# Ranks of edges from keys along the free dimension in place of transposed one-hots

## The chip, the cores and the metric

One core of a Trainium2 chip runs the whole program. The metric is the device time of one execution in microseconds. TensorE (PE), VectorE (DVE), ScalarE (ACT), GpSimd (POOL) and SyncE (SP) run their own instruction streams and meet at semaphores; data moves between DRAM and SBUF by DMA.

## The reference, cut to what matters

Four graph layers follow each other on 12,500 nodes of 32 features and 200,000 edges (padded to 128 x 1568). Edges come sorted by destination, not by source. The last layer needs sums over the edges of each source, so the kernel sorts the edges by source itself. Nothing in the reference is called a rank; what matters of it is

```python
edge_index = jnp.stack([src, dst])
...
x = x + _L1_gnn_ref(h, edge_index, 12500)      # msgs = x[src]; out = segment_sum(msgs, dst)
...
x = x + _L3_gnn_ref(h, edge_index, L3_gnn_w, L3_gnn_fc_w, L3_gnn_fc_b, L3_gnn_bias)
# in it: seg_max, seg_sum and segment_sum over src
```

The rank of an edge is its place in the order by source: the number of edges with a smaller source, plus the number of earlier edges with the same source.

## The kernel before

The 1568 columns of edges are handled in chunks of 16 (`CH`), a chunk holds 128 x 16 edges, and a chunk is ranked in four groups of four columns (`GR`, `GROUPS`). The edges are in two lists by the parity of their chunk, `ROWS` and `PTRS`, with 49 chunks (`PAIRS`) each. A key is split into `lo` (key mod 128) and `hi` (key div 128, 98 values). VectorE makes two one-hots of a chunk, `hot_lo` 128 x 16 x 128 (L1095) and `hot_hi` 128 x 16 x 98 (L1097), by comparing with `iota_ps`, a row of numbers in PSUM. A table `place_ps`, 128 x 98, holds for each key where its next edge goes; it starts from the prefix sums of the counts, and each group adds its own edges (`hot_lo` transposed times `hot_hi`).

For a group the kernel before does this (class `Ranks`). TensorE transposes the four `hot_lo` (L1002); ScalarE copies the result twice, to bf16 and to f32 (L1067, L1068). TensorE multiplies the transposed one-hots with each other, which tells which edges share `lo`: four blocks within a column, with a triangle added so that only earlier rows count (L1035, L1038), and three calls between columns (L1042). ScalarE copies these (L1081, L1082). TensorE counts the group on into `place_ps` (L1049, L1051), ScalarE copies that (L1085), and TensorE then makes for each of the four columns a 128 x 98 product of table and equal keys (L1011, L1014, L1015) in which VectorE picks each edge's `hi` and adds up (L1110). The order of TensorE's calls in `group` is: turn the next group, equal keys of this one, count on, ranks of the group before.

Ranks are made in two stages. In the early one (destination softmax, first layer) GpSimd gathers the rows `en` (L1218), 32 a pair of chunks; `keep_step` holds the gather at every eighth row until `counted` or `R.ranked` has come so far. TensorE and VectorE first count all keys, then rank 14 chunks (`AHEAD`), 56 groups; ScalarE waits for all of them before it begins the loop over edges (L1417 and after). In the late stage (second layer) GpSimd gathers the rows `hs` by source, 16 to an iteration (L1627), into one of two buffers; it waits on `laid`, which ScalarE raises when it has copied the buffer of two iterations before (L1742). Of the 98 iterations the first 13 (`MID`) hold 4 count chunks each (L1704), the other 85 one ranked chunk, 84 in all (`RANKED`), 336 groups. There ScalarE's order in an iteration is: `mask`, the four groups (`count_on`), the copy at L1742, `store`. VectorE's is: the last two groups' picks of the chunk before, `keep`, the next one-hots, the first two groups' picks, then `add_up` (a carry, a scan over 512 elements at L718). Semaphores and program order alone set the order; no planner is involved. `K.wait` issues waits; `Chain` numbers VectorE's own steps. Elsewhere nothing is touched.

Of the kernel before, what the change touches and what calls it, by code (L numbers as in the profile page):

```python
# [4 lines left out]
F32 = mybir.dt.float32  # L5
# [24 lines left out]
GROUPS = CH // GR  # L30
BIG = 1.0e30
# [139 lines left out]
def build(nc, A, out):  # L171
    top = ExitStack()
    with top:
# [54 lines left out]
        sums = dram("sums", (EDGES, FEAT))  # L228

# [730 lines left out]
        class Ranks:  # L960
# [3 lines left out]
            def __init__(self, st, which, chunks, iota, then=None, after=None):  # L964
                self.which, self.plan, self.iota, self.then, self.after = which, chunks, iota, then, after
                self.hot_lo = [sb(st, f"hot_lo{k}", [EP, CH, 128], BF16) for k in range(2)]
                self.hot_hi = [sb(st, f"hot_hi{k}", [EP, CH, NB], BF16) for k in range(2)]
                self.hot_t = [sb(st, f"hot_t{q}", [NP, GR, EP]) for q in range(GROUPS)]
                self.hot_tb = [sb(st, f"hot_tb{q}", [NP, GR, EP], BF16) for q in range(GROUPS)]
                self.place_sb = [sb(st, f"place_sb{q}", [NP, NB]) for q in range(GROUPS)]  # L970
                self.own_same = [sb(st, f"own_same{k}", [EP, GR, EP], BF16) for k in range(2)]
                self.cross_same = [sb(st, f"cross_same{k}", [EP, 2, 3 * EP], BF16) for k in range(2)]
                self.not_before = sb(st, "not_before", [EP, GR, EP], BF16)
                self.picked = sb(st, "picked", [EP, GR, NB])
                self.pos = [sb(st, f"pos{k}", [EP, CH]) for k in range(2)]

                turn_bank = ps(st, "turn_bank", [NP, 512])
                self.turn_ps = turn_bank[:, 0:GR * 64].bitcast(BF16).rearrange("p (g e) -> p g e", g=GR)
                self.place_ps = turn_bank[:, 384:384 + NB]
                self.own_ps = ps(st, "own_ps", [EP, GR, EP])  # L980
                self.cross_ps = ps(st, "cross_ps", [EP, 2, 512])
                self.rank_ps = [ps(st, f"rank_ps{k}", [EP, GR, NB]) for k in range(2)]
                (self.hots, self.turned, self.turned_sb, self.samed, self.copied_same, self.ranked, self.selected, self.placed,
                 self.place_out, self.triangle) = (K.sem(n) for n in (
                     "rank_hots", "rank_turned", "rank_turned_sb", "samed", "copied_same", "ranked", "selected", "counts_placed",
                     "place_out", "triangle"))
# [5 lines left out]
            def cross(self, a, b):  # L992

                return (0, (b - 1) * EP) if a == 0 else (1, (b - 2 if a == 1 else 2) * EP)
# [3 lines left out]
            def turn(self, pe, n, k, q):  # L998

                K.wait(pe, "pe", self.turned_sb, n, self.place_out, n)  # L1000
                for g in range(GR):
                    last = nc.tensor.transpose(self.turn_ps[:, g, 0:EP], self.hot_lo[k][:, q * GR + g, :], identb[0:EP, 0:EP])  # L1002
                last.then_inc(self.turned, 1)

            def rank(self, pe, n, k, q):

                s = q % 2
                K.wait(pe, "pe", self.selected, GR * (n - 1), self.copied_same, n + 1)
                for b in range(GR):
                    o = self.rank_ps[s][:, b, :]  # L1010
                    nc.tensor.matmul(o, self.hot_t[q][:, b, :], self.place_sb[q][:, :], start=True, stop=False)  # L1011
                    for a in range(b):
                        bank, at = self.cross(a, b)
                        nc.tensor.matmul(o, self.cross_same[s][:, bank, at:at + EP], self.hot_hi[k][:, q * GR + a, :], start=False, stop=False)  # L1014
                    last = nc.tensor.matmul(o, self.own_same[s][:, b, :], self.hot_hi[k][:, q * GR + b, :], start=False, stop=True)  # L1015
                last.then_inc(self.ranked, 1)

            def begin_pe(self, pe):

                pe.wait_ge(self.triangle, 1)  # L1020
                K.wait(pe, "pe", self.hots, 1)
                self.turn(pe, 0, 0, 0)

            def group(self, pe, r, k, q, last_chunk):

                n = r * GROUPS + q
                more = q < GROUPS - 1 or not known_ge(r, last_chunk)
                if q < GROUPS - 1:
                    self.turn(pe, n + 1, k, q + 1)
                elif more:  # L1030
                    K.wait(pe, "pe", self.hots, r + 2)
                    self.turn(pe, n + 1, 1 - k, 0)
                K.wait(pe, "pe", self.turned_sb, n + 1, self.copied_same, n)
                hot_tb = self.hot_tb[q]
                nc.tensor.matmul(self.own_ps[:, :, :].rearrange("p g e -> p (g e)"), identb[0:EP, 0:EP],  # L1035
                                 self.not_before[:, :, :].rearrange("p g e -> p (g e)"), start=True, stop=False)
                for a in range(GR):
                    nc.tensor.matmul(self.own_ps[:, a, :], hot_tb[:, a, :], hot_tb[:, a, :], start=False, stop=a == GR - 1)  # L1038
                for a in range(GR - 1):
                    bank, at = self.cross(a, a + 1)  # L1040
                    later = hot_tb[:, a + 1:GR, :].rearrange("p c e -> p (c e)")
                    last = nc.tensor.matmul(self.cross_ps[:, bank, at:at + (GR - 1 - a) * EP], hot_tb[:, a, :], later, start=True, stop=True)  # L1042
                last.then_inc(self.samed, 1)

                if more:
                    K.wait(pe, "pe", self.place_out, n + 1, self.turned_sb, n + 2)
                else:
                    K.wait(pe, "pe", self.place_out, n + 1)
                nc.tensor.matmul(self.place_ps, ident[:, :], self.place_sb[q][:, :], start=True, stop=False)  # L1049
                for g in range(GR):  # L1050
                    last = nc.tensor.matmul(self.place_ps, self.hot_lo[k][:, q * GR + g, :], self.hot_hi[k][:, q * GR + g, :],  # L1051
                                            start=False, stop=g == GR - 1)
                last.then_inc(self.placed, 1)

                if q:
                    self.rank(pe, n - 1, k, q - 1)
                elif not first_chunk(r):
                    self.rank(pe, n - 1, 1 - k, GROUPS - 1)

            def end_pe(self, pe, last_chunk):  # L1060
                self.rank(pe, last_chunk * GROUPS + GROUPS - 1, last_chunk % 2, GROUPS - 1)
# [3 lines left out]
            def take_turned(self, act, n, q):  # L1065
                K.wait(act, "act", self.turned, n + 1, self.ranked, n - (GROUPS - 1))
                nc.scalar.copy(self.hot_tb[q][:, :, :], self.turn_ps[:, :, 0:EP])  # L1067
                nc.scalar.copy(self.hot_t[q][:, :, :], self.turn_ps[:, :, 0:EP]).then_inc(self.turned_sb, 1)  # L1068

            def begin_act(self, act):  # L1070
                nc.scalar.copy(self.place_sb[0][:, :], base_src[self.which][:, :]).then_inc(self.place_out, 1)
                self.take_turned(act, 0, 0)

            def count_on(self, act, r, k, q, last_chunk):

                n, s = r * GROUPS + q, q % 2
                if q < GROUPS - 1 or not known_ge(r, last_chunk):
                    self.take_turned(act, n + 1, (q + 1) % GROUPS)
                K.wait(act, "act", self.samed, n + 1, self.ranked, n - 1)

                nc.scalar.activation(self.own_same[s][:, :, :], self.own_ps[:, :, :], ACT.Relu)  # L1081
                nc.scalar.copy(self.cross_same[s][:, :, :], self.cross_ps[:, :, 0:3 * EP]).then_inc(self.copied_same, 1)  # L1082
                K.wait(act, "act", self.placed, n + 1, self.ranked, n - (GROUPS - 2))
                turning = self.after is not None and n + 1 == self.after * GROUPS
                nc.scalar.copy(self.place_sb[(q + 1) % GROUPS][:, :], base_src[self.then][:, :] if turning else self.place_ps).then_inc(self.place_out, 1)  # L1085

            def start(self):
# [65 lines left out]
        with ExitStack() as st:  # L1155
# [84 lines left out]
            def _(act):  # L1240
# [28 lines left out]
                def rank_ahead(i):  # L1269
                    for k in range(2):  # L1270
                        for q in range(GROUPS):
                            R.count_on(act, 2 * i + k, k, q, AHEAD - 1)
# [1401 lines left out]
```

## Time and profile before

| what | value |
|---|---|
| three runs | 12865.76, 12874.27, 12892.65 us; median 12874.27 |
| profiled execution | 12867.33 us |
| its span | 12865.4 us |
| mean granted TensorE clock | 0.638 |
| busy: PE / weight loads | 5229.5 us (41%) / 3057.0 us |
| busy: DVE, ACT, POOL | 7050.3 (55%), 3858.4 (30%), 7257.5 us (56%) |

The times are of executions; the span is from the first to the last instruction of the profiled one. Busy shares are means over very different stages. A granted clock of 1 is 2.4 GHz and 0.5 is 1.2 GHz. An f32 matmul is shown as two records. "issue" and "remote" name idle time for which the profile has no releaser.

### The profile page before, as it was taken

Reading aid. Unit: us, or ns where it says so; the run is one execution under the profiler, and the core shown is the slowest. Engines: PE = TensorE matmul, PEld = TensorE weight load, DVE = VectorE, ACT = ScalarE, POOL = GpSimd, SP = SyncE. Lnnn points to the kernel's source line nnn. Section 1 sums busy time; section 2 is a strip of 40 time slices with the busy share of each in tenths; the row PEclk is TensorE's granted clock in tenths of the full one; section 3 lists DMA queues with packets and bytes.
Section 4 is the critical chain, followed back from the end, with each engine's and each line's share of the span. In section 5 each row is a group of like instructions: output and inputs, shape, how many; then the busy total and the mean of one; then the engine's idle time right before and its main releaser. Section 6 shows DMA issues by size and latency. Waiting matters only on the chain. (4 is left out here: it accounts for less than half of the span.)

```text
span 12865.4 us, 86012 instructions
## 1 busy us (share of the span) xinstructions
PE 5229.5 (41%) x25371; PEld 3057.0 (24%) x25371; DVE 7050.3 (55%) x11102; ACT 3858.4 (30%) x6150; POOL 7257.5 (56%) x7431
## 2 busy tenths in 40 slices
PE   2225300038135555555537777777514343400001
PEld 1214300012134444444423222222211111100001
DVE  4754588888442222222227777677515555567761
ACT  0002333345023333333312222222102333356640
POOL 5645677748554444444456655555563555566654
PEclk5556655569556666666657777777657666655555
DMA  6101366634300000000011111111110111133331
GB/s 237 46 20 40 129 216 213 214 141 157 109 18 16 17 17 15 17 17 17 15 31 24 25 23 23 23 24 23 20 16 4 46 30 31 33 93 126 123 102 39
DMA packets 464212, 813.80 MB, mean 63 GB/s; under 512 B 227109, under 2 KB 324822, under 8 KB 413446
## 3 DMA queue, kind: packets, MB, share of 16 engines
q10 hardware_dynamic: 81456, 446.55, 8.9%
q0 software_dynamic: 234304, 156.53, 7.0%
q1 hardware_dynamic: 147990, 205.22, 4.9%
q8 instruction: 209, 3.42, 0.1%
q14 instruction: 253, 2.07, 0.1%
HBM read 401.53 MB, written 406.14 MB: 63 GB/s over the span
## 5 line engine op out<-in xcount | busy, mean ns | idle before, releaser
L1627 POOL DMA_INDIRECT hs<-tab_h,src_i x3136 | 2973.0, 948 | 2764.7 <-issue 1224.2
L1218 POOL DMA_INDIRECT en<-tab_s,src_i x1568 | 1571.0, 1002 | 827.8 <-issue 493.6
L1110 DVE SCALAR_TENSOR_TENSOR picked<-rank_ps,hot_hi 128x98 f32<-128x98 f32 x1568 | 313.3, 256 | 2106.2 <-remote 1146.8
L1912 PE MATMUL tp_ps<-w_pair,x 128*128 128x512 f32 x1568 | 1075.1, 774 | 435.4 <-DVE prod_b L2050 377.6
L2332 POOL DMA_INDIRECT rows_src<-out_rows,pos x784 | 754.2, 962 | 775.8 <-ACT out_rows L2378 503.2
L2357 PE MATMUL late_ps<-hot_col,hot_row 128*128 128x512 bf16 x1248 | 590.9, 486 | 1097.0 <-DVE hot_col L2456 670.0
L2456 DVE TENSOR_SCALAR hot_col<-count_up,pos_late 128x784 bf16<-128x784 f32 x624 | 628.1, 1030 | 726.8 <-remote 576.7
L2344 POOL DMA_INDIRECT hs<-tab_h,ptr x784 | 743.0, 948 | 367.1 <-issue 256.0
L1011 PE MATMUL rank_ps<-place_sb,hot_t 128*128 128x98 f32 x3136 | 868.6, 394 | 0.0
L2047 DVE TENSOR_TENSOR prod_a<-tp_ps,zz 128x768 f32<-128x768 f32 x392 | 374.7, 956 | 701.2 <-remote 478.6
L1011 PEld LDWEIGHTS rank_ps<-place_sb,hot_t 128*128 128x128 f32 x3136 | 705.5, 277 | 3.3
L1049 PE MATMUL turn_bank<-place_sb,ident 128*128 128x98 f32 x784 | 236.5, 397 | 1029.1 <-ACT hot_t L1068 623.9
L1067 ACT COPY hot_tb<-turn_bank 128x512 bf16<-128x512 bf16 x392 | 229.1, 584 | 1231.4 <-remote 889.8
L1095 DVE TENSOR_TENSOR hot_lo<-iota_ps,lo_s 128x2048 bf16<-128x2048 f32 x196 | 448.5, 2288 | 247.0 <-remote 230.5
L2387 ACT ACTIVATE hot_row<-row_flags,late_high 128x128 bf16<-128x128 bf16 x624 | 244.1, 391 | 1055.1 <-DVE row_flags L2453 553.4
L1318 PE MATMUL cnt_ps<-hot_hi,hot_lo 128*128 128x98 bf16 x2352 | 218.8, 282 | 739.0 <-DVE hot_hi L1097 542.0
L836 PE MATMUL turn<-ident,tot 128*2 128x128 f32 x2 | 0.7, 372 | 1261.6 <-DVEq L872 1261.6
L2357 PEld LDWEIGHTS late_ps<-hot_col,hot_row 128*128 128x128 bf16 x1248 | 140.0, 112 | 1498.3 <-issue 761.5
L2144 PE MATMUL turn<-ident,both 128*33 128x128 f32 x16 | 3.6, 421 | 1180.0 <-issue 1180.0
L660 DVE TENSOR_TENSOR_SCAN run<-keep,fresh 128x2244 f32<-128x2244 f32 x98 | 473.2, 4828 | 0.5 <-issue 0.3
L729 ACT COPY rows<-run 128x512 f32<-128x512 f32 x294 | 311.7, 1060 | 481.7 <-DVE run L718 390.5
L1912 PEld LDWEIGHTS tp_ps<-w_pair,x 128*128 128x128 f32 x1568 | 297.9, 230 | 664.5 <-issue 554.3
(408 smaller groups left out, 16290.9 us busy)
## 6 DMA issues: line engine op xcount, KB each, us to landing
sums<-rows ACTq DMA_DIRECT2D x98, 1088.0 KB
sums<-rows ACTq DMA_DIRECT2D x147, 512.0 KB
ev_rows<-zeros ACTq DMA_DIRECT2D x16, 3136.0 KB
raw<-ev_rows ACTq DMA_DIRECT2D x49, 1024.0 KB
r<-in_edge_attr_2x ACTq DMA_DIRECT2D x49, 1024.0 KB
y_rows<-r ACTq DMA_DIRECT2D x49, 1024.0 KB
y<-y_rows SPq DMA_DIRECT2D x49, 1024.0 KB
hs<-tab_h,src_i POOLq DMA_INDIRECT x3136
```

What stands on the lines that cost most here:

```text
L660: nc.vector.tensor_tensor_scan(flat(self.run[k][:, :, :]), flat(self.keep[k][:, :, :]), flat(self.fresh), 0.0, ALU.mult, ALU.add).then_inc ...
L1011: nc.tensor.matmul(o, self.hot_t[q][:, b, :], self.place_sb[q][:, :], start=True, stop=False)
L1095: nc.vector.tensor_tensor(self.hot_lo[k][:, :, :], self.iota[:, 0:128].unsqueeze(1).to_broadcast([EP, CH, 128]), lo[:, cols(t)].unsqueeze( ...
L1110: nc.vector.scalar_tensor_tensor(self.picked[:, g, :], self.rank_ps[q % 2][:, g, :], 1.0, self.hot_hi[k][:, at, :], ALU.mult, ALU.mult, ac ...
L1218: pool.indirect_dma_start(en[s][:, g, :], None, tab_s0, bass.IndirectOffsetOnAxis(ap=src_i[:, p * 2 * CH + g:p * 2 * CH + g + 1], axis=0)) ...
L1627: pool.indirect_dma_start(rows[k][:, g, :], None, tab_h, bass.IndirectOffsetOnAxis(ap=src_i[:, t * CH + g:t * CH + g + 1], axis=0)).then_i ...
L1912: nc.tensor.matmul(o, x2[k][:, a, b * EP:(b + 1) * EP], w3_cols, start=True, stop=False)
L2047: made[q] = c.mark(nc.vector.tensor_tensor(prod_a[q % 2][:, :, :, :], wts[:, :, :, 0:3 * MUL], zz[k][:, four, :, :].rearrange("p c n u -> ...
L2332: pool.indirect_dma_start(rows_src, bass.IndirectOffsetOnAxis(ap=pos2[s][:, g:g + 1], axis=0), out_rows[s][:, g, :], None).then_inc(sent_r ...
L2344: pool.indirect_dma_start(rows[PTRS][s][:, g, :], None, tab_h3, bass.IndirectOffsetOnAxis(ap=ptr[:, i * CH + g:i * CH + g + 1], axis=0)).t ...
L2357: nc.tensor.matmul(late_ps[:, 0:512], flags, hot_col[n % 2][:, 0:512], start=begins, stop=ends)
L2456: nc.vector.tensor_scalar(hot_col[n % 2][:, :], count_up, pos_late[:, n:n + 1], None, ALU.is_equal).then_inc(late_hot, 1)
```

## The change

The transposed one-hots and the products between them go. Instead the source keys are also loaded transposed (`src_t`, laid out on the host side of the launch like the other inputs), split by VectorE into `lo` and `hi` in the early stage, and stored as two rows of bf16 in DRAM (`lh_rows`). For each chunk a small load brings 2 x 2048 of them (`fetch`: by the ScalarE queue early, by SyncE late).

Per group TensorE spreads the two rows over all partitions with matmuls of two rows (`widen`), ScalarE takes the distance from the partition's number and turns it into one-hots by `Abs` and `Relu` (`lift`), `lo` and `hi` side by side. The table is split into two bf16 halves (`place`, ScalarE and VectorE) and looked up for all 512 edges (`look_ps`); VectorE multiplies with the `hi` one-hots (`part`). For equal keys TensorE spreads the whole key (`row`), and VectorE compares it with the keys of each column (`own`, `later`). Three matmuls with one-row selectors (`add_up`) add everything into one row of `pos_ps`; every 16 groups (`BATCH`) the rows are copied, turned back and stored. In the late stage ScalarE's `lay` and `store` and VectorE's `add_up` of an iteration move between the groups of the next.

```diff
+BATCH = 16
...
+        lh_rows = dram("lh_rows", (2, EDGES), BF16)
...
+            def fetch(self, eng, who, r):
+                K.wait(eng, who, self.rowed, GROUPS * (r - 1))
+                at = self.chunk(r) * CH * EP
+                eng.dma_start(self.key_rows[r % 2][:, :], lh_rows[:, at:at + CH * EP]).then_inc(self.keys_in[r % 2], 16)
...
+            def widen(self, pe, n):
...
+                K.wait(pe, "pe", self.lifted, n)
+                nc.tensor.matmul(self.wide_ps[:, 0, :], self.parts[:, 0, :], self.key_row(n), start=True, stop=True)
+                nc.tensor.matmul(self.wide_ps[:, 1, :], self.parts[:, 1, :], self.key_row(n), start=True, stop=True).then_inc(self.widened, 1)
+            def row(self, pe, n):
+                K.wait(pe, "pe", self.sames, n)
+                nc.tensor.matmul(self.row_ps[:, :], self.parts[:, 2, :], self.key_row(n), start=True, stop=True).then_inc(self.rowed, 1)
+            def add_up(self, pe, n):
...
+                nc.tensor.matmul(self.pos_ps[:, :], self.selectb[:, at], self.own[n % 2][:, :], start=m == 0, stop=False)
+                nc.tensor.matmul(self.pos_ps[:, EP:GR * EP], self.selectb[:, at], self.later[n % 2][:, :], start=False, stop=False)
+                nc.tensor.matmul(self.pos_ps[:, :], self.select[0:NB, at], self.part[n % 2][:, :], start=False, stop=last).then_inc(self.ranked, 1)
...
+            def group_pe(self, pe, n):
...
+                if more:
+                    self.widen(pe, n + 1)
+                K.wait(pe, "pe", self.split, n + 1)
...
+                nc.tensor.matmul(self.look_ps[:, :], place[:, 0, :], self.hot_t[n % 3][:, 0, :], start=True, stop=False)
+                nc.tensor.matmul(self.look_ps[:, :], place[:, 1, :], self.hot_t[n % 3][:, 0, :], start=False, stop=True).then_inc(self.looked, 1)
...
+                    nc.tensor.matmul(self.place_ps, identb[:, :], place[:, 0, :], start=True, stop=False)
+                    nc.tensor.matmul(self.place_ps, identb[:, :], place[:, 1, :], start=False, stop=False)
+                    for g in range(GR):
+                        last = nc.tensor.matmul(self.place_ps, self.hot_lo[k][:, q * GR + g, :], self.hot_hi[k][:, q * GR + g, :],
+                                                start=False, stop=g == GR - 1)
+                    last.then_inc(self.counted, 1)
+                if n:
+                    self.add_up(pe, n - 1)
+                if more:
+                    self.row(pe, n + 1)
...
+            def lift(self, act, n):
+                K.wait(act, "act", self.widened, n + 1, self.halved, n - 1)
+                nc.scalar.activation(self.away[n % 2][:, :, :], self.wide_ps[:, :, :], ACT.Abs, bias=self.minus_p[:, 0:1]).then_inc(self.lifted, 1)
+                K.wait(act, "act", self.lifted, n + 1, self.picked, n - 2)
+                nc.scalar.activation(self.hot_t[n % 3][:, :, :], self.away[n % 2][:, :, :], ACT.Relu, scale=-1.0, bias=ones[:, 0:1])
...
+            def group_act(self, act, n):
+                K.wait(act, "act", self.counted, n + 1)
+                nc.scalar.copy(self.place[n % 2][:, 0, :], self.place_ps).then_inc(self.halved, 1)
+                if n + 1 < self.groups:
+                    self.lift(act, n + 1)
...
+            def group_dve(self, dve, c, n):
...
+                nc.vector.tensor_tensor(place[:, 1, :], self.place_ps, place[:, 0, :], ALU.subtract).then_inc(self.split, 1)
...
+                K.wait(dve, "dve", self.rowed, n + 1, self.ranked, n - 1)
...
+                    nc.vector.scalar_tensor_tensor(own[:, at], self.row_ps[:, at], key[:, q * GR + g:q * GR + g + 1], before[0:EP, 0:EP],
+                                                   ALU.is_equal, ALU.mult)
...
+                first = c.mark(nc.vector.tensor_scalar(later[:, :], self.row_ps[:, EP:], key[:, q * GR:q * GR + 1], None, ALU.is_equal))
...
+                K.wait(dve, "dve", self.looked, n + 1)
+                nc.vector.tensor_tensor(self.part[n % 2][:, :], self.look_ps[:, :], self.hot_t[n % 3][0:NB, 1, :], ALU.mult).then_inc(self.picked, 1)
...
+                c.step(nc.vector.tensor_scalar(bits[:, :], keys_t, 127, None, ALU.bitwise_and))
+                c.step(nc.vector.tensor_copy(lo_d[:, :], bits[:, :]))
+                c.step(nc.vector.tensor_scalar(bits[:, :], keys_t, 7, None, ALU.arith_shift_right))
+                c.step(nc.vector.tensor_copy(hi_d[:, :], bits[:, :]))
...
-                    S.mask(act, t, k)
-                    if 0 <= r < RANKED:
-                        for q in range(GROUPS):
-                            R.count_on(act, r, r % 2, q, RANKED - 1)
-                    K.wait(act, "act", gathered[k], p * (16 * CH) + 16 * CH, S.scanned, t)
-                    nc.scalar.copy(S.message(k), rows[k][:, :, :].rearrange("p c f -> p f c")).then_inc(laid, 1)
-                    S.store(act, t, k, p)
+                    if r < RANKED:
+                        R.group_act(act, r * GROUPS)
+                        R.group_act(act, r * GROUPS + 1)
...
+                    if r:
+                        lay(t - 1)
+                    if r < RANKED:
+                        R.group_act(act, r * GROUPS + 2)
+                    if r:
+                        S.store(act, t - 1, (t - 1) % 2, (t - 1) // 2)
+                    if r < RANKED:
+                        R.group_act(act, r * GROUPS + 3)
+                    S.mask(act, t, t % 2)
```

## Rows read from the trace of the kernel before

**Rows 1.** Busy by stretches (us from:to, length, engines, clock, DMA): early ranks, late ranks

```profile
1084.00:1471.00 387.00, 250.86 (x2012) 220.16 (x2012) 99.16 (x493) 139.72 (x281) 204.29 (x216) 0.72 0.14 35
...
3723.40:6536.70 2813.30, 1557.43 (x12092) 1358.82 (x12092) 745.39 (x3191) 1037.63 (x1934) 1255.92 (x1328) 0.68 0.08 16
```

**Rows 2.** Line L1049 alone, late and early (ns min/median/max, first and last start)

```profile
L1049 PE MATMUL turn_bank<-place_sb,ident x672: 275/421/504, 3725.9 to 6530.2; 128*128 128x98 f32 x168
...
L1049 PE MATMUL turn_bank<-place_sb,ident x112: 275/421/504, 1086.8 to 1460.4; 128*128 128x98 f32 x112
```

**Rows 3.** Waits of 3740 to 6520 us (us in total, times, longest)

```profile
DVE picked L1110 <- remote: 1044.6, 127, 10.7
POOL hs L1627 <- ACT fresh L1742: 973.0, 71, 14.8
```

**Rows 4.** Busy by stretches: a gather, the pause after it, a gather while counting, five iterations

```profile
5017.94:5037.63 19.69, 6.51 (x45) 5.53 (x44) 6.99 (x20) 5.12 (x9) 15.12 (x16) 0.66 0.16 40
5037.63:5051.94 14.31, 13.16 (x102) 11.73 (x103) 1.93 (x18) 7.31 (x14) 0.00 (x1) 0.63 0.01 2
3406.20:3425.90 19.70, 5.95 (x64) 5.10 (x64) 17.30 (x11) 4.01 (x5) 15.09 (x16) 0.50 0.88 333
...
3406.20:3528.70 122.50, 29.76 (x320) 25.49 (x320) 86.45 (x56) 12.98 (x16) 75.67 (x81) 0.50 0.57 211
```

**Rows 5.** Timeline, late ranks (start, length, what, idle time before and its releaser)

```profile
5025.96 0.28 PE L1015 MATMUL rank_ps<-hot_hi,own_same 128*128 128x98 bf16 x1
...
5029.94 0.26 DVE L1110 SCALAR_TENSOR_TENSOR picked<-rank_ps,hot_hi 128x98 f32<-128x98 f32 x1 [9.77 <-remote]
...
5041.10 0.28 PE L1015 MATMUL rank_ps<-hot_hi,own_same 128*128 128x98 bf16 x1
...
5041.43 0.26 DVE L1110 SCALAR_TENSOR_TENSOR picked<-rank_ps,hot_hi 128x98 f32<-128x98 f32 x1 [6.45 <-PE rank_ps L1015]
...
5051.94 0.94 POOL L1627 DMA_INDIRECT hs<-tab_h,src_i  x1 [14.31 <-ACT fresh L1742]
...
5053.72 0.26 DVE L1110 SCALAR_TENSOR_TENSOR picked<-rank_ps,hot_hi 128x98 f32<-128x98 f32 x1 [0.56 <-DVE fresh L712]
...
5074.82 0.26 DVE L1110 SCALAR_TENSOR_TENSOR picked<-rank_ps,hot_hi 128x98 f32<-128x98 f32 x1 [7.89 <-PE rank_ps L1015]
```

**Rows 6.** Timeline, counting in the late stage

```profile
3406.23 0.94 POOL L1627 DMA_INDIRECT hs<-tab_h,src_i  x1 [17.66 <-PE cnt_ps L1704]
...
3518.97 2.29 DVE L1095 TENSOR_TENSOR hot_lo<-iota_ps,lo_s 128x2048 bf16<-128x2048 f32 x1 [21.20 <-remote]
...
3528.67 0.94 POOL L1627 DMA_INDIRECT hs<-tab_h,src_i  x1 [14.40 <-PE cnt_ps L1704]
```

**Rows 7.** Timeline of TensorE at a granted clock of 0.5

```profile
5008.51 0.63 PE L1035 MATMUL own_ps<-not_before,identb 128*128 128x512 bf16 x1
5008.94 0.63 PE L1038 MATMUL own_ps<-hot_tb 128*128 128x128 bf16 x4
...
8008.05 2.05 PE L1912 MATMUL tp_ps<-w_pair,x 128*128 128x512 f32 x2 [4.77 <-DVE prod_b L2050]
8010.03 0.60 PE L1913 MATMUL tp_ps<-b_rows,ones_b 3*128 3x512 bf16 x1
```

**Rows 8.** Timeline of VectorE: the two compares of a chunk

```profile
3528.66 2.29 DVE L1095 TENSOR_TENSOR hot_lo<-iota_ps,lo_s 128x2048 bf16<-128x2048 f32 x1
3530.87 1.78 DVE L1097 TENSOR_TENSOR hot_hi<-iota_ps,hi_s 128x1568 bf16<-128x1568 f32 x1
```

**Rows 9.** Groups of instructions, ScalarE (busy us, mean ns, idle before)

```profile
L729 ACT COPY rows<-run 128x512 f32<-128x512 f32 x294 | 311.7, 1060 | 481.7 <-DVE run L718 390.5 <-DMA sums<-rows 57.7 <-issue 33.4
...
L1742 ACT COPY fresh<-hs 128x512 f32<-128x512 f32 x98 | 106.5, 1087 | 27.4 <-DMA hs<-tab_h,src_i 27.4
...
L1085 ACT COPY place_sb<-turn_bank 128x98 f32<-128x98 f32 x391 | 103.3, 264 | 26.1 <-remote 24.9
L1292 ACT ACTIVATE fifth<-zw 128x1024 f32<-128x1024 f32 x98 | 100.4, 1024 | 706.3 <-issue 485.8 <-DVE zw L1417 220.4
```

**Rows 10.** Line L533 alone: the table loads before a root

```profile
L533 ACT ACT_TABLE_LOAD  x3: 1283/1283/1283, 15.4 to 9258.1; - x3
```

**Rows 11.** Line L1218 alone, 1080 to 1480 us, and what ended its waits

```profile
L1218 POOL DMA_INDIRECT en<-tab_s,src_i x224: 942/947/957, 1097.3 to 1480.0; - x112
...
  PE rank_ps L1015: 122.8, 23
```

More of the change, by code:

```diff
@@ L960, in build, with __init__ @@
         class Ranks:
-            def __init__(self, st, which, chunks, iota, then=None, after=None):
-                self.which, self.plan, self.iota, self.then, self.after = which, chunks, iota, then, after
+            def __init__(self, st, which, chunks, iota_bank, batches, then=None, after=None, pos_sb=None):
+                self.which, self.plan, self.then, self.after = which, chunks, then, after
+                self.iota = iota_bank[:, 0:128]
+                self.targets = [target for _, target in batches]
+                self.at = [(b, m, m == size - 1) for b, (size, _) in enumerate(batches) for m in range(size)]
+                self.groups = GROUPS * len(chunks)
@@ L972, in __init__ @@
[L972 to L986, printed above, removed]
+                self.keys = [sb(st, f"keys{k}", [EP, CH]) for k in range(2)]
@@ new lines, in __init__ @@
+                self.later = [sb(st, f"later{n}", [EP, (GR - 1) * EP], BF16) for n in range(2)]
+                self.part = [sb(st, f"part{n}", [NB, GR * EP]) for n in range(2)]
+                self.select = sb(st, "select", [EP, 2 * BATCH - 1])
+                self.selectb = sb(st, "selectb", [EP, 2 * BATCH - 1], BF16)
+                self.pos_sb = sb(st, "pos_sb", [BATCH, GR * EP]) if pos_sb is None else pos_sb
+                bank = ps(st, "place_bank", [NP, 512])
+                self.place_ps = bank[:, 0:NB]
@@ L988, in chunk @@
+                self.keys_in = [K.sem(f"keys_in{k}") for k in range(2)]
             def chunk(self, r):
                 return self.plan[r]
[L992 to L1000, printed above, removed]
-                for g in range(GR):
-                    last = nc.tensor.transpose(self.turn_ps[:, g, 0:EP], self.hot_lo[k][:, q * GR + g, :], identb[0:EP, 0:EP])
-                last.then_inc(self.turned, 1)
@@ L1005, in rank @@
[L1005 to L1016, printed above, removed]
@@ L1018, in begin_pe @@
-            def begin_pe(self, pe):
[L1020 to L1043, printed above, removed]
-                if more:
-                    K.wait(pe, "pe", self.place_out, n + 1, self.turned_sb, n + 2)
-                else:
[L1048 to L1058, printed above, removed]
@@ L1074, in count_on @@
[L1074 to L1085, printed above, removed]
@@ new lines, in turn_back @@
+            def turn_back(self, pe, b):
+                K.wait(pe, "pe", self.pos_out, b + 1, self.pos_kept, b)
+                for g in range(GR):
+                    last = nc.tensor.transpose(self.back_ps[:, g, :], self.pos_sb[:, g * EP:(g + 1) * EP], ident[0:BATCH, 0:BATCH])
+                last.then_inc(self.pos_back, 1)
+            def begin_pe(self, pe):
+                pe.wait_ge(self.ready, 1)
+                nc.tensor.matmul(self.place_ps, ident[:, :], base_src[self.which][:, :], start=True, stop=True).then_inc(self.counted, 1)
+                self.widen(pe, 0)
+                self.row(pe, 0)
@@ L1331, in _ @@
                 R.begin_pe(pe)
-                def rank_ahead(i):
-                    for k in range(2):
-                        for q in range(GROUPS):
-                            R.group(pe, 2 * i + k, k, q, AHEAD - 1)
-                pairs(rank_ahead, end=AHEAD // 2)
-                R.end_pe(pe, AHEAD - 1)
+                for n in range(AHEAD * GROUPS):
+                    R.group_pe(pe, n)
+                R.end_pe(pe)
                 softmax.pe(pe)
```

267 lines of the change are left out of this document (170 added, 97 removed).

## The prediction

> **What bounds the kernel now.** I read the view by stretches first. The ranks are worked out in two places. The late one, in the stage that gathers `hs`, runs from 3723.4 to 6536.7 us; TensorE, VectorE, ScalarE and GpSimd are busy there for 1557, 745, 1038 and 1256 us of 2813 [rows 1]. No engine fills it. The early one runs from 1084 to 1471 us [rows 1]. L1049 issues two matmul records per group of four columns, so its x672 and x112 are 336 groups late and 56 early [rows 2]. A chunk has four groups: 84 chunks late, 2813.3 / 84 = 33.5 us each; 387 / 56 = 6.9 us a group early.
>
> Second, the waits of the late stretch: VectorE's picks wait longest, much of it for a releaser the profile can't name, and GpSimd waits 973 us for ScalarE's copy at L1742 [rows 3]. So GpSimd isn't the bound; its gather is held until the rows buffer is emptied, which stands behind four groups in ScalarE's order.
>
> Third, one chunk cut in two. In the 19.7 us of a gather TensorE issues 45 matmul records, in the 14.3 us after it 102 [rows 4]. The timeline shows how that looks. Within the gather the last matmul of a rank is recorded at 5025.96 for 0.28 us, and the pick, which has nothing else to wait for, starts at 5029.94, 3.7 us late; after the gather the rank recorded at 5041.10 is over at 5041.38 and its pick starts at 5041.43 [rows 5]. The picks of the two groups after it end with the one at 5053.72, 12.3 us later, and the next rank to come through the following gather (begun at 5051.94) with the pick at 5074.82 is 22.9 us behind that begin [rows 5]. So of 33.5 us two groups take 12 outside and two take some 21.5 with the gather. GpSimd had waited 14.3 us for its start [rows 5].
>
> Fourth, the same stage before its ranks, where TensorE only counts: four count chunks of 16 matmuls stand beside each 16 gathers. Here TensorE issues 64 records in 19.7 us of gather, and VectorE is busy only 86 of 122.5 us [rows 4]. Five iterations take 3528.67 - 3406.23 = 122.4 us, 24.5 each; before the last, GpSimd waits 14.4 us for a count, and one compare waits 21.2 us [rows 6]. I read both places alike: a gather leaves TensorE a budget, and pauses of GpSimd pay for what is over it.
>
> **The change, late stage.** *TensorE, records.* A group had 4 turns, 5 + 3 for equal keys, 2 + 4 to count on and 18 for ranks, 36 matmul records and as many weight loads. It gets 2 (widen), 2 (look), 6 (count on), 4 (add up: two bf16 and one f32, which shows as two), 1 (row): 15. Per chunk 60 in place of 144, plus eight short ones every 16 groups.
>
> *TensorE, time.* A 512-column bf16 matmul at the lower clock starts 0.43 us before the next (5008.51 to 5008.94); an f32 one of 512 columns 1.98 us (8008.05 to 8010.03) [rows 7]. So six of 512, one of 384 (0.32), six of 98 (0.08 each) and the f32 one: 2.58 + 0.32 + 0.49 + 1.98 = 5.4 us a group at 1.2 GHz, half at 2.4, 4.3 at the 0.63 granted after the gather; the 102 records there, busy 13.16 us, make 4.6 for 36 [rows 4]. The array time hardly changes; the count of instructions does. The mean clock of the stretch is 0.68, between the two levels [rows 1].
>
> *VectorE.* Compares of 2048 and 1568 elements from PSUM take 2.29 and 1.78 us, and the second starts 2.21 after the first [rows 8]: 1.06 ns an element + 0.05. New per group: 98 (0.16), 384 (0.46), four of 128 (0.20 each), 256 (0.33), 128 (0.20), 512 (0.60): 2.55 us, with waits 2.7, in place of four picks (0.7). The trace has no compare against a pointer column summed into bf16; bounds are 0.18 us, one pick's step, and twice the value for each, 1.4 to 5.1 a group; I take 2.7, as all read PSUM like the row. Per chunk 4 x 2.7 + 3.9 (one-hots, unchanged) + 0.1 (keys) + 1.9 (sums) = 16.7 us of 33.5: beside TensorE, not the bound.
>
> *ScalarE.* Out go two copies of 512, own and cross. In come Abs and Relu of 1024, at 1.02 each, and the copy of 98, 0.26 [rows 9]: 2.3 us a group. Chunk: 9.2 + 2.7 for mask (about half a copy of 512), lay (1.09) and store (1.06) [rows 9] = 11.9 us. All beside TensorE. Relu and copies alternate now without a table load; Abs is not in the trace. Between no load and one of 1.283 us [rows 10] at each turn, 8 a chunk or 10.3 us, I take none; even then ScalarE's 22.2 us stay under the chunk below.
>
> *Order and queues.* Lay and store move between groups one and two of the next iteration: GpSimd starts no later relative to the ranks, with a buffer's slack. SyncE's key fetches (8 KB, 84 of them) stand behind zero fills that end before the ranks; each is asked for three groups ahead. ScalarE queue in the early stage does the same. They cost nothing under that cover; I have no row of such a small load, and if each came 2 us late, the one-hot wait would grow by 84 x 2 = 168.
>
> *Chunk time.* Needed: 60 records. A gather lets through 45 (as now) to 64 (as in counting). With 64 the chunk goes as counting does: 24.5 us. With 45, three groups pass until 22.9 us after the gather's begin [rows 5] and one follows at 5.4: 28.3 us. Middle 26.4. Saving 84 x (33.5 - 26.4) = 596 us. VectorE's upper bound (5.1 a group, 26.3 a chunk) ends at the same place; its lower one changes nothing. The next limit is then GpSimd, 16 gathers of 1.25 us, 20.0.
>
> **Early stage.** The gathers are gated by ranks: 224 of them, 122.8 us of waits for rank_ps [rows 11]. 28 pairs of groups at 13.8 us; a pair now brings 30 records, not 72, for 8 gathers (10.0 us at least). Between 10.0 and 13.8 I take 12.4, as hops stay: 28 x 1.4 = 40 us. Bounds 107 saved, or 60 lost if VectorE's part doubles. The loop after it starts when ranks end and is bound by VectorE, so the gain passes on. The four new 1568-element passes (about 5 us) and 1.6 MB more DMA fall where VectorE waits for counts; at worst +10 us.
>
> **Sum.** Profiled execution 12867.3 us (span 12865.4 and 1.9 around it): 12867 - 596 - 40 = 12231, say 12230. The shown median, 12874.3, is 7 higher; within what I can tell.
>
> **A rule weighed.** The late pick of rows 5 and the 45 against 102 records of rows 4 say that TensorE's results are held up while GpSimd gathers. The Trainium skill, SBUF — State Buffer (Who interferes with whom), states the opposite: ScalarE and TensorE never wait on anyone, and a DMA never contends with a compute engine. By that rule nothing but GpSimd's own pace would be left and the result would be the floor rival's below. The trace disagrees, with 3.7 us.
>
> **Rivals.**
> *Held up by time, not by count.* If a gather lets through array time, not records, two groups pass as now and two follow at 5.4: 21.5 + 10.8 = 32.3 us. 12867 - 84 x 1.2 - 20 = 12746. For it: array time per group is unchanged. Against: counting passed 64 records with 16 x 4 x 0.08 = 5 us of array time in the same gather where ranks passed 45 with some 7.
> *GpSimd's floor.* 60 records fit, groups run at 4 us (VectorE 2.7 + one-hots 1.0), the chunk is 20.1 us: 12867 - 84 x 13.4 - 106 = 11635. For it: 60 < 64. Against: counting, with looser waits, did not get below 24.5.
> *Late completions in series: slower.* VectorE now waits in one group for three results of TensorE in turn (row, look, count). If each comes 3.7 us late during a gather, a group takes 2.7 + 11.1 = 13.8 us, 1.7 pass in 22.9 us and 2.3 follow at 5.6: 35.8 us, + 84 x 2.3 = 193; early a pair takes 20, + 28 x 6.2 = 174: 13234. It decides from about 3 us of lateness on each of the three. Against: TensorE does look, count and row in one batch, and late results come together.
> *It doesn't do what it says*: ranks that VectorE still compares and TensorE still adds; the record counts must fall from 36 to 15 a group, or nothing follows.
>
> **How the numbers follow.** Forecast (chunk 23.5 to 29) 0.50; held by time 0.20; floor 0.14; slower 0.13; no change 0.03. A difference under 0.2% (26 us) can't be told from none. Faster 0.84, same 0.03, slower 0.13. The range goes from a chunk of 22 (12867 - 966 - 60 = 11841) to just past the second case, 12780.
>
> **What would show it.** L1049's successor at 336 and 56 groups; late stretch 84 x 26.4 = 2218 us, not 2813; early about 347, not 387. TensorE records in it 336 x 15 + 21 x 8 = 5208, from 12092. VectorE busy 1400 us there. GpSimd's wait for the `hs` copy down from 14.3 to about 6.5 us a chunk. Wrong, if VectorE's busy share passes 0.8 (its terms mis-sized), if the chunk stays above 30 at 15 records a group (hold-up by time), or if picks of a group trail in three steps (series).

## The result and the profile after

The changed kernel takes 12531.27 us (median; 12515.23 to 12538.61) against 12870.01 us (12845.44 to 12892.65): ratio 0.973, 95% interval 0.9714 to 0.9745. It is faster by some 340 us, where 644 were forecast. The profiled execution took 12537.5 us with a span of 12535.4, 330 less than before.

Busy time by stretches of the changed kernel, columns as in [rows 1]: early ranks, late ranks, one gather of 16 rows, and the pause of GpSimd after it.

```profile
1085.00:1430.00 345.00, 250.02 (x849) 77.22 (x850) 226.85 (x547) 137.04 (x171) 194.87 (x207) 0.66 0.15 39
3685.00:6172.00 2487.00, 1494.14 (x5115) 462.03 (x5114) 1502.25 (x3544) 1026.62 (x1278) 1247.64 (x1320) 0.65 0.08 18
4958.32:4978.03 19.71, 10.99 (x47) 3.54 (x45) 9.91 (x28) 6.68 (x9) 15.13 (x16) 0.76 0.16 40
4978.03:4988.31 10.28, 5.06 (x15) 1.39 (x14) 7.32 (x13) 5.57 (x6) 0.00 (x0) 0.50 0.01 2
```

The late ranks fell from 2813 to 2487 us [rows 1]: 2487 / 84 = 29.6 us a chunk, from 33.5. The early ones fell from 387 to 345, or 12.3 us a pair of groups. Together that is 368 us, of which 330 reach the end of the kernel. TensorE's records went from 12092 to 5115, and VectorE's work doubled, from 745 to 1502 us. Under the gather shown TensorE issues 47 records, and 15 in the pause after it. The 45 and 102 of [rows 4] were not typical of the kernel before: over 82 late gathers of each trace I count 59 records a gather and 85 a pause before, 46 and 15 after the change. Two gathers of the kernel before, the next ones after that of [rows 4]:

```profile
5051.94:5071.65 19.71, 8.73 (x58) 7.57 (x56) 7.00 (x20) 5.02 (x9) 15.13 (x16) 0.67 0.10 14
5084.45:5104.16 19.71, 9.32 (x68) 8.32 (x66) 7.00 (x20) 5.02 (x9) 15.13 (x16) 0.71 0.15 40
```

Waits of the changed kernel in 3740 to 6150 us (total, times, longest), beside [rows 3]:

```profile
POOL hs L1708 <- ACT fresh L1819: 691.9, 70, 12.5
...
DVE place L1153 <- ACT place L1109: 282.4, 80, 8.0
...
DVE later L1169 <- remote: 208.4, 75, 6.5
```

GpSimd still waits for ScalarE's copy of the rows, now some 10 us a chunk (692 us with that name, the rest under "issue"). The timeline of the same gather's successor (begun at 4988.31, over at 5008.0) shows on what all else waits. First TensorE, then who waits for it:

```profile
4997.07 0.38 PE L1064 MATMUL look_ps<-hot_t,place 128*98 128x512 bf16 x1
4997.29 0.21 PE L1069 MATMUL place_bank<-place,identb 128*128 128x98 bf16 x1
...
4997.38 0.34 PE L1072 MATMUL place_bank<-hot_hi,hot_lo 128*128 128x98 bf16 x4
```

```profile
5008.76 0.24 ACT L1109 CAST place<-place_bank 128x98 bf16<-128x98 f32 x1 [7.74 <-remote]
5010.96 1.11 ACT L1092 ACTIVATE away<-wide_ps,minus_p 128x1024 bf16<-128x1024 f32 x1 [1.95 <-remote]
```

The count at L1072 is recorded as over at 4997.72, ScalarE's copy of it starts at 5008.76: 11 us late. Taking the times at which the semaphores rise from the trace, I find that TensorE's alone are late. Those of ScalarE and VectorE rise 0.01 us after the instruction's end, under a gather too; TensorE's do so for the first 20 to 30 records of a gather (over 81 gathers the first late one is number 26 to 30 in the middle half). Record 28 to 30 then comes mostly at 10 to 12 us, record 36 at about 20, and what is later comes in one batch, 0.04 us apart, 2.8 us after the gather's last instruction. In the kernel before the same holds for its records: number 30 at 10 to 12 us, 34 at 15 to 17, 42 at 22.5.

### The profile page after: what moved, and what is told of

Its sections match the earlier page's. It is cut to its first block and busy times, and to the rows that moved or that the text cites. A ratio compares the mean times of both kernels' runs of the same rounds, so it can differ in the third digit from the quotient of the medians.

```text
span 12535.4 us, 67678 instructions
## 1 busy us (share of the span) xinstructions
PE 5167.8 (41%) x17243; PEld 2013.4 (16%) x17243; DVE 7936.3 (63%) x11527; ACT 3850.4 (31%) x5390; POOL 7259.0 (58%) x7431
## 5 line engine op out<-in xcount | busy, mean ns | idle before, releaser
L1092 ACT ACTIVATE away<-wide_ps,minus_p 128x1024 bf16<-128x1024 f32 x392 | 436.9, 1115 | 2000.3 <-PE wide_ps L1023 1379.6
L1038 PE MATMUL pos_ps<-part,select 98*16 98x512 f32 x784 | 611.6, 875 | 0.0
L1063 PE MATMUL look_ps<-hot_t,place 128*98 128x512 bf16 x392 | 225.1, 574 | 820.9 <-DVE place L1153 439.4
L1153 DVE TENSOR_TENSOR place<-place_bank,place 128x98 bf16<-128x98 f32 x392 | 100.5, 256 | 606.3 <-ACT place L1109 320.2
L1161 DVE SCALAR_TENSOR_TENSOR own<-row_ps,keys,before 128x128 bf16<-128x128 f32 x1568 | 470.6, 342 | 0.0
L1094 ACT ACTIVATE hot_t<-away,ones 128x1024 bf16<-128x1024 bf16 x392 | 449.8, 1148 | 12.8
L1169 DVE TENSOR_SCALAR later<-row_ps,keys 128x384 bf16<-128x384 f32 x392 | 240.0, 612 | 307.1 <-remote 238.0
L2448 PE MATMUL late_ps<-hot_col,hot_row 128*128 128x272 bf16 x1248 | 430.7, 345 | 0.0
```

What stands on the lines that cost most here:

```text
L1038: nc.tensor.matmul(self.pos_ps[:, :], self.select[0:NB, at], self.part[n % 2][:, :], start=False, stop=last).then_inc(self.ranked, 1)
L1094: nc.scalar.activation(self.hot_t[n % 3][:, :, :], self.away[n % 2][:, :, :], ACT.Relu, scale=-1.0, bias=ones[:, 0:1])
L1161: nc.vector.scalar_tensor_tensor(own[:, at], self.row_ps[:, at], key[:, q * GR + g:q * GR + g + 1], before[0:EP, 0:EP], ALU.is_equal, ALU. ...
```

## The experiments

Two conditions have to be kept apart. In the runs of the result, in the first set and in the third set (the three sets ran on three chips) TensorE's results come late under gathers, and the kernel before takes 12,845 to 12,956 us. On the chip of the second set they don't, and the same kernel takes 9791.87 us. Comparisons below stay within a chip unless the text says otherwise; numbers of stages are read from each run's trace, between the first and the last count of the ranks, over 83.75 chunks.

**First set: what holds TensorE up.** Plain loads in place of the gathers, for the changed kernel and for the one before:

```diff
+            def plain(eng, t, k):
+                for g in range(CH):
+                    eng.dma_start(rows[k][:, g, :], tab_h[g * EP:(g + 1) * EP, :]).then_inc(plain_in[k], 16)
...
+                for t in range(MID, 2 * PAIRS):
+                    K.wait(sp, "sp", laid, t - 1)
+                    gather.plain(sp, t, t % 2)
```

> The changed kernel, but in the 85 iterations with ranks the rows hs come by 16 plain loads of the SyncE queue (same bytes, same 128-byte pieces, a fixed place of the table) in place of GpSimd's 16 gathers; which rows are read is left out, so the sums are not the reference's. Held up by GpSimd's gathers (my theory): the results of TensorE come without delay, a chunk takes its own chain, four groups at 4 to 4.5 us and the one-hots at 4.1, 20 to 22 us in place of 29.6, the late ranks 1680 to 1850 us in place of 2487, the kernel about 11,750 to 11,900. Held up by the traffic into SBUF (rival): the same traffic, so 28 us a chunk or more. Not held up, a chain of VectorE and ScalarE alone: 29 us, unchanged.

> The kernel before with the same plain loads in place of GpSimd's gathers in the ranked iterations. Theory: groups take the 6 us that they take outside a gather, so 24 us a chunk in place of 33.5, late ranks about 2020 us in place of 2813. If the change's gain of 3.9 us a chunk comes from fewer instructions under the gather, it should be smaller here, 2 to 3 us between this kernel and its changed twin; if it comes from a shorter chain, it stays 3.9 or grows. Traffic as the cause: 32 us or more.

Late ranks, new and old with plain loads:

```profile
3638.80:5348.90 1710.10, 1351.16 (x5105) 434.45 (x5103) 1487.12 (x3535) 1021.07 (x1275) 0.00 (x0) 0.75 0.12 27
```

```profile
3672.90:5242.80 1569.90, 1180.00 (x12042) 1040.10 (x12041) 731.46 (x3169) 1015.70 (x1923) 0.00 (x0) 0.89 0.13 29
```

The changed kernel took 11708.37 us, the old one 11611.63, beside 12900.28 for the kernel before. A chunk takes 20.4 us in the new and 18.75 in the old one. So the gathers cost the old kernel 33.5 - 18.75 = 14.7 us a chunk and the new one 29.6 - 20.4 = 9.2, with 33.5 and 29.6 from the traces of the result, as neither kernel was traced with gathers in this set. The same bytes by another queue delay nothing, and in more pieces: the trace shows a gather as 16 packets of 1024 bytes and 16 of 4, a plain load as 128 of 128 bytes and 16 of 4. So it is not the amount of traffic into SBUF. What is left is all that a gather of GpSimd has and a load of SyncE has not, its scattered rows of the table too; which of it, the pair doesn't tell. And I had expected the old kernel at 24 us, behind the new one; it is 1.7 us a chunk ahead. Without gathers the change is a loss (97 us in one run of each, 0.8%), and its whole gain is that the gathers hurt it less. The changed kernel's 11,708 us is just under the 11,750 expected.

Array time or number of records, in `add_up` of the late ranks:

```diff
+                    nc.tensor.matmul(self.pos_ps[0:BATCH - 1, :], self.select[0:NB, 0:BATCH - 1], self.part[n % 2][:, :], start=False, stop=False)
```

> The changed kernel with one more f32 matmul of 512 columns per group in the late ranks (weights of zero, so nothing changes in the sums): 2 more records a group, 17 in place of 15, but 2 us more array time at 1.2 GHz, 1 us at 2.4. A gather lets through a number of records (theory): 8 more of 63 a chunk, plus what lies on the path outside the gather: 1 to 2.5 us a chunk, 30.6 to 32. It lets through array time (rival): 6 to 8 us a chunk, 36 or more.

```diff
+                    for _ in range(8):
+                        nc.tensor.matmul(self.pos_ps[0:BATCH - 1, 0:2], self.selectb[:, 0:BATCH - 1], identb[0:EP, 0:2], start=False, stop=False)
```

> The changed kernel with eight more bf16 matmuls of two columns per group in the late ranks (weights of zero): 23 records a group in place of 15, about 0.9 us more array time at 1.2 GHz. By number of records (theory): the some 45 records of a gather are two groups in place of three, the third goes after it: 3.5 to 5 us a chunk more, 33 to 34.5. By array time (rival): 1 us a chunk more, at most 31.

Late ranks of the two:

```profile
3686.40:6207.30 2520.90, 1674.17 (x5773) 500.10 (x5771) 1501.95 (x3533) 1021.80 (x1275) 1244.52 (x1319) 0.74 0.09 18
```

```profile
3672.70:6306.00 2633.30, 1621.11 (x7777) 533.35 (x7775) 1500.68 (x3531) 1024.80 (x1275) 1246.14 (x1318) 0.63 0.09 17
```

They took 12606.51 and 12702.45 us. A chunk takes 30.1 us with the long matmul and 31.4 with the eight short ones. The changed kernel alone, not run in this set, takes 29.6 in the runs of the result and 30.3 in the third set, so the long one costs at most 0.5 us, less than I had expected, and the short ones 1.1 to 1.8. TensorE's busy time is 1674 and 1621 us in place of 1494. The long matmul added less to it than its length says, since the granted clock of the stretch was 0.74 beside 0.65: net 180 us, 2.1 us a chunk. Array time as the budget would have cost about that, and 6 to 8 us by my expectation; at most 0.5 was measured. Nor is it constant: a gather holds 8.3 us of TensorE's busy time on average in the kernel before, 12.9 in the changed one and 14.1 with the long matmul. The count matters, but costs less than half of what I had expected. With eight more, the first late record is number 31 to 39 in the middle half of the gathers, with the long matmul number 23 to 31; and a gather lets through 63 and 51 records on average. So what is roughly fixed, to some ten records, is where the delay begins, not how many records a gather lets TensorE issue: one group's records go in a row once its inputs are there, and the next group waits for the late result. Counting [rows 4] fits this and no fixed 45: it needs nothing back from TensorE but a buffer.

**Second set, on a chip without the delay.** Three orders and a pacing of the gathers:

```diff
                 nc.vector.tensor_tensor(place[:, 1, :], self.place_ps, place[:, 0, :], ALU.subtract).then_inc(self.split, 1)
+                if between is not None:
+                    between()
...
-                        R.group_dve(dve, c, r * GROUPS)
-                        if r + 1 < RANKED:
-                            R.hot(dve, r + 1)
+                        R.group_dve(dve, c, r * GROUPS, next_hot if r + 1 < RANKED else None)
```

> The changed kernel, with VectorE's one-hots of the next chunk (4.1 us) moved from behind a chunk's first group to behind its split of the table, where VectorE waits 3.8 us for TensorE's late results anyway. Theory (the one-hots stand on the path of the chunk, which I had put beside TensorE): 3 to 4 us a chunk less, 26 to 26.7 in place of 29.6, kernel about 12,250 to 12,300. Rival (TensorE's budget under the gather is all that counts): unchanged, 29 to 30.

```diff
                         R.group_act(act, r * GROUPS)
-                        R.group_act(act, r * GROUPS + 1)
...
                         lay(t - 1)
                     if r < RANKED:
+                        R.group_act(act, r * GROUPS + 1)
                         R.group_act(act, r * GROUPS + 2)
```

> The changed kernel, with ScalarE's copy of the gathered rows one group earlier, so that the next gather starts 3 to 4 us sooner after the last one. Theory (pauses of GpSimd pay for what TensorE can't do under a gather): what the gather wins TensorE loses, 28.5 to 30 us a chunk. Rival (the cycle is gather plus ScalarE's way to the copy): 25.5 to 26.5.

```diff
+                    S.mask(act, t, t % 2)
...
+                        for q in range(GROUPS):
+                            R.group_act(act, r * GROUPS + q)
...
+                    lay(t)
+                    S.store(act, t, t % 2, t // 2)
```

> The changed kernel with ScalarE's lay and store and VectorE's sums back at the end of the same iteration, as in the kernel before. Theory: the order of ScalarE decides when a gather starts, not how much TensorE does in a chunk: 29 to 30.5 us. Rival (the moved order brought the gain): 33 us and more, the kernel back at 12,850.

```diff
-    K.wait(pool, "pool", R.ranked, min(GROUPS * (t - MID - 2) + quarter, GROUPS * RANKED))
+    K.wait(pool, "pool", R.ranked, max(0, min(GROUPS * (t - MID - 1) + quarter + 1, GROUPS * RANKED)))
```

> The changed kernel, with the late gathers let go four at a time, one group of ranks behind each four (as the early stage does with eight), in place of 16 in one go. Theory (TensorE goes on without delay for some 30 records after a gather begins, and is given back its pace in a pause): each four gathers of 5 us meet one group of 15 records, results are not held up, and a chunk takes 24 to 26 us. Rival (each gather costs TensorE the same, wherever it stands): 29 to 30.5; or slower, since a gather now waits for ranks and ranks for the gather: 31 and more.

They took 9840.97, 9833.57, 10108.05 and 9838.22 us, beside 9791.87 for the kernel before. All four expectations presupposed the delay, so none was tested; the pacing and the moved one-hots were run again with it in the third set, the earlier copy and the old order were not. What the set does show: the late ranks of the paced kernel, and two rows in the midst of its gathers.

```profile
3096.00:4808.90 1712.90, 1354.09 (x5106) 435.96 (x5103) 1486.75 (x3535) 1021.10 (x1275) 1258.40 (x1334) 0.75 0.12 27
3606.42:3626.40 19.98, 15.68 (x61) 5.09 (x60) 17.38 (x42) 11.78 (x16) 15.04 (x16) 0.74 0.16 40
```

```profile
3615.70 0.53 PE L1072 MATMUL place_bank<-hot_hi,hot_lo 128*128 128x98 bf16 x4
3616.26 0.24 ACT L1109 CAST place<-place_bank 128x98 bf16<-128x98 f32 x1 [2.29 <-PE place_bank L1072]
```

In 20 us, 16 gathers and 61 records pass, ScalarE's copy follows the count 0.03 us after its end, and a chunk takes 20.4 us in three of the four kernels: the same as with plain loads. That number is the chain of the new ranks; GpSimd's floor of 20.0 lies just below it. Only the old order of ScalarE and VectorE is different, 23.8 us: there the moved `lay`, `store` and sums are worth 3.4 us a chunk. That is nearly the 3.9 us that the change gains where results come late, and there the old order was not run: how much of the 3.9 us is the new order and how much the fewer records stays open. The changed kernel itself did not run on this chip. Its three nearest relations, with the same 20.4 us, were 42 to 49 us slower than the kernel before, one run each: the gain of 2.7% is not there.

**Third set, with the delay.**

> The changed kernel itself once more. In the last set the kernel before took 9791.87 us where it had taken 12,870 to 12,900, and no result of TensorE came late under a gather: either the chip delays them or it doesn't. Where it delays them: 12,515 to 12,540, ratio 0.973, late chunk 29.6 us. Where it doesn't (theory: fewer TensorE instructions then gain nothing, and the longer chain of the changed kernel shows): 9,820 to 9,860, ratio 1.002 to 1.007, slower, late chunk 20.4 us. Rival (fewer instructions help everywhere): ratio 0.99 or less in both.

> The changed kernel with the late gathers let go four at a time, one group of ranks behind each four. Where results come late: theory (some 30 records pass without delay after a gather's begin, and a pause gives the pace back) 24 to 26 us a late chunk, kernel 12,060 to 12,230; rival (each gather costs the same wherever it stands) 29 to 30.5. Where they don't: 20.4 us, as it was.

> The changed kernel with VectorE's one-hots of the next chunk behind the split of the first group. Where TensorE's results come late: theory (the one-hots are on the chunk's path) 26 to 26.7 us a late chunk; rival (only TensorE's budget counts) 29 to 30. Where they don't: 20.4, as it was.

> The kernel before, with a trace on the same chip as the three others. Where results come late: late chunk 33.5 us as known. Where they don't: its chain alone is 18.75 us a chunk (with plain loads), so GpSimd's 16 gathers set the pace, 20.0 to 20.3 us, late ranks about 1690 us; early pair about 9 us as in the changed kernel or a little less.

Late ranks of the changed kernel, of the paced one, of the one with moved one-hots and of the kernel before, in this order:

```profile
3691.60:6226.00 2534.40, 1474.77 (x5105) 457.62 (x5103) 1496.32 (x3532) 1024.52 (x1275) 1243.18 (x1318) 0.66 0.08 18
```

```profile
3687.80:5795.00 2107.20, 1534.04 (x5106) 469.37 (x5104) 1490.72 (x3535) 1016.19 (x1275) 1254.04 (x1330) 0.66 0.10 22
```

```profile
3688.00:5968.30 2280.30, 1468.06 (x5105) 448.54 (x5104) 1500.17 (x3536) 1014.97 (x1275) 1243.49 (x1318) 0.67 0.09 20
```

```profile
3746.80:6549.90 2803.10, 1475.81 (x11877) 1308.28 (x12043) 741.25 (x3169) 1028.30 (x1923) 1252.76 (x1328) 0.69 0.08 16
```

| kernel | us | ratio (95%) | late chunk | early pair |
|---|---|---|---|---|
| before | 12920.86 (7 runs) | | 33.5 | 14.2 |
| changed | 12637.25 (12602.61 to 12658.21) | 0.9791 (0.9760 to 0.9821) | 30.3 | 12.4 |
| one-hots moved | 12360.72 (one run) | | 27.2 | 12.4 |
| paced | 12184.41 (12183.53 to 12187.02) | 0.9436 (0.9409 to 0.9462) | 25.2 | 12.9 |

The changed kernel comes out 100 us higher on this chip than in its first runs, at a ratio of 0.979 where I had expected 0.973 again; its late chunk is 0.6 us longer. The moved one-hots give 3.0 us a chunk, at the low end of the 3 to 4 expected (27.2 us is above the 26.7 expected, as the changed kernel has 30.3 here): they did stand on the path. VectorE's rows show how it is with them, in the wait for the late results:

```profile
4605.81 0.26 DVE L1153 TENSOR_TENSOR place<-place_bank,place 128x98 bf16<-128x98 f32 x1 [4.79 <-ACT place L1109]
4606.06 2.28 DVE L1134 TENSOR_TENSOR hot_lo<-iota_ps,lo_s 128x2048 bf16<-128x2048 f32 x1
4608.26 1.78 DVE L1136 TENSOR_TENSOR hot_hi<-iota_ps,hi_s 128x1568 bf16<-128x1568 f32 x1
4612.65 0.62 DVE L1171 TENSOR_SCALAR later<-row_ps,keys 128x384 bf16<-128x384 f32 x1 [2.62 <-remote]
```

Pacing gives 5.1 us, within the 24 to 26 expected, and is the best version here, 3.6% below the changed kernel and 5.6% below the kernel before. GpSimd's waits show the trade:

```profile
POOL hs L1708 <- PE pos_ps L1038: 407.3, 134, 9.0
...
POOL hs L1708 <- ACT fresh L1819: 7.2, 4, 3.0
```

It waits in short pieces for ranks and hardly ever for the emptied buffer (691.9 us in the changed kernel), and fewer of TensorE's results fall into the long delay; some still do, up to 9.0 us. Pacing and moved one-hots together, and either with the kernel before, were not run.

## Why the prediction was right, and where it missed

**The direction and the place.** The diagnosis held: the 3.7 us of lateness [rows 5] come with GpSimd's gathers, and plain loads remove them in both kernels. That the change helps because it issues fewer instructions is in part argued: eight more records a group cost 1.1 to 1.8 us a chunk, so the count has a price, but the change also moved `lay`, `store` and the sums, and the two were not taken apart where results come late. The Trainium skill's rule (SBUF — State Buffer, Who interferes with whom), by which TensorE waits for no one, described the chip of the second set and not the others; by it I would have forecast 11635 on a chip that gives 12531. It is stated for the ports of SBUF, and whether a port has a part in the late results no run shows.

**The late chunk, 26.4 forecast, 29.6 measured.** This term missed: the late ranks gained 326 us of the 596 forecast. The step "a gather lets through 45 to 64" failed. The 45 was one gather of a kernel that lets through 59 on average, and there is no such budget: the changed kernel lets through 46, with eight more a group 63. What the traces show is a delay that begins after some 20 to 35 records and then holds up whatever waits for a result. The bound of 45 gave 28.3, three groups by 22.9 us and one at 5.4, and came nearest. That three groups pass is as measured, but the 45 that it was worked out from was no measure of it, so that much is luck. The 22.9 us held: the batch of late results lands 22.5 to 22.6 us after a gather's begin. The fourth group was the other mis-sized term: from the batch at 4980.9 to the next gather at 4988.31 it takes 7.4 us, not 5.4. In it ScalarE lifts twice (1.1 and 1.15 us each time), waits, and copies the rows (1.0), while VectorE makes 4.1 us of one-hots between two groups. So the step "beside TensorE, not the bound" for VectorE and ScalarE failed. Their sums of work were small enough, but both are links of a chain that runs when TensorE has just been let go. Moving the one-hots gave 3.0 us back. ScalarE's share is read from these rows alone; no run with late results moved its steps.

**VectorE's durations.** `own` took 0.342 us, not 0.20, the first `later` 0.61, not 0.46, `part` 0.68, not 0.60. Its late total was 1502 us, forecast 1400; the group came to 3.1 us, within the bounds 1.4 to 5.1.

**The early stage.** 12.3 us a pair against 12.4 forecast, 42 us against 40. The 12.4 was picked between 10.0 and 13.8, so the hit is partly luck. Here the gathers are let go eight at a time, a pacing like that which the third set gave to the late stage; where results are not late a pair takes 9.0 us.

**TensorE's records** came to 5115 for 5208 forecast, the array time to much the same as before (1494 and 1557 us), GpSimd's pause to 10.2 us a chunk on average (10.3 in the one shown) for 6.5.

**The rivals.** Held up by array time is refuted: at most 0.5 us a chunk for 2.1 us of busy time more, and gathers that hold 8.3 us of it in one kernel and 12.9 in the other. GpSimd's floor stands where results are not late (20.4 us a chunk against 20.1). Late completions in series did happen, in the gather shown in one group of four. Its three results of TensorE (look, count, row) let VectorE and ScalarE go on one after the other:

```profile
4970.33 0.69 DVE L1179 TENSOR_TENSOR part<-look_ps,hot_t 98x512 f32<-98x512 f32 x1 [1.26 <-remote]
4976.68 0.24 ACT L1109 CAST place<-place_bank 128x98 bf16<-128x98 f32 x1 [5.70 <-issue]
4980.99 0.62 DVE L1169 TENSOR_SCALAR later<-row_ps,keys 128x384 bf16<-128x384 f32 x1 [3.77 <-remote]
```

That is the sign that I had named for this rival. Its price was wrong, not its mechanism: two groups of the chunk pass before the delay begins (5.1 and 4.6 us), only the other two take 10.5 and 10.8, and what is still out ends with the batch. The slower side that I didn't name: the chain of the new ranks is 1.7 us a chunk longer than that of the old ones, which shows wherever nothing holds TensorE up.

**What stays open.** Why TensorE's results came late on some chips and not on another, and by what GpSimd's indirect loads delay them, no run shows; nor whether it is the chip or its state at the time, as the three sets ran on a chip each. The traces themselves differ too: that of the paced kernel has 149,298 rises of semaphores on the chip without the delay and 45,724 on one with it, and all with gathers and delay have 43,000 to 46,000. The kernel makes the same rises in each, so many went unrecorded there; whether the recording has a part in the delay no run shows either. That the delay begins after some 20 to 35 records was seen in the kernel before, the changed one and its two variants with more matmuls, not taken apart. And the share of the moved steps in the gain is open, as said.

## What to carry to other kernels

When an engine's results come late only while another engine does one kind of work, measure the kernel with that work replaced before you restructure: here it told that the new algorithm is longer and only better shielded. Interleave the disturbing work with the disturbed in small portions before you thin out the instructions; one changed wait brought more (3.6%, on top of the change) than the rewritten ranks (2.1% on the same chip). And an engine with time to spare is not off the path if its work stands between two links of the chain.

## What was unexpected of the hardware

The same kernel took 12,900 us on one chip and 9,792 on another, at mean granted clocks of 0.64 and 0.71. Late results of TensorE under GpSimd's indirect loads were the difference that the traces show, in stages other than the ranks too: the changed kernels reached their late ranks at 3,097 us in place of 3,688. A verdict on such a kernel holds for the condition in which it was measured.
